# A fused attention and expert kernel: layer-norm statistics of x placed half a batch ahead, routing of a finished batch gathered in the first head group

## The reference, cut to what matters

```python
def _layernorm(x, axis=-1, eps=1e-05):
    m = jnp.mean(x, axis=axis, keepdims=True)
    v = jnp.var(x, axis=axis, keepdims=True)
    return (x - m) / jnp.sqrt(v + eps)
...
scores = jnp.einsum('bhqd,bhkd->bhqk', q, k) * scale
attn = jax.nn.softmax(scores, axis=-1)
out = jnp.einsum('bhqk,bhkd->bhqd', attn, v)
...
vals, idx = jax.lax.top_k(probs, K)
gates = mask / (jnp.sum(mask, axis=-1, keepdims=True) + EPS)
h = jax.nn.gelu(jnp.einsum('bsd,edh->besh', x, W1) + b1, approximate=False)
y = jnp.einsum('bse,besd->bsd', gates, jnp.einsum('besh,ehd->besd', h, W2) + b2)
...
x = x + xattn(_layernorm(x), ctx)
x = x + ffn(_layernorm(x))
```

## Time and profile before

| what | value |
|---|---|
| time, median of 3 runs | 816.91 us |
| lowest, highest | 812.75 us, 820.35 us |
| the profiled execution: its own time | 811.37 us |
| the profiled execution: its span | 809.6 us |
| PE busy | 751.9 us (93%) |
| DVE busy | 612.4 us (76%) |
| ACT busy | 455.7 us (56%) |
| POOL busy | 393.1 us (49%) |
| PE's mean granted clock | 0.966 |

### The profile page before, as it was taken

One profiled execution on the slowest core, in us unless ns is written; L12 is line 12 of the kernel. 1 busy time (PEld: TensorE's weight loads), 2 busy tenths in 40 slices (PEclk: granted clock), 3 DMA queues, 4 the chain that ended last, 5 costly groups with the idle time before them and its releaser, 6 DMA issues.

```text
span 809.6 us, 16188 instructions
## 1 busy us (share of the span) xinstructions
PE 751.9 (93%) x4634; PEld 449.7 (56%) x4634; DVE 612.4 (76%) x1123; ACT 455.7 (56%) x663; POOL 393.1 (49%) x354
## 2 busy tenths in 40 slices
PE   7689999999999999999999988759999989999995
PEld 3333434444444444444443433338999879998994
DVE  6586687788788788788788788536786887777674
ACT  1146766766766776776766756744345334444441
POOL 6406125628728728728725604243444455344444
PEclk9669999999999999999999999979999999999998
DMA  5765766757767767757757668874444555454441
GB/s 184 220 164 169 203 171 222 202 184 253 209 196 254 209 191 253 203 182 249 214 169 249 169 161 291 276 241 96 75 94 74 85 128 111 71 79 71 71 74 12
DMA packets 90667, 136.23 MB, mean 168 GB/s; under 512 B 15464, under 2 KB 49224, under 8 KB 90200
## 3 DMA queue, kind: packets, MB, share of 16 engines
q1 hardware_dynamic: 76456, 116.80, 48.0%
q0 software_dynamic: 13296, 17.09, 12.1%
q10 hardware_dynamic: 832, 1.31, 0.5%
HBM read 71.25 MB, written 64.04 MB: 167 GB/s over the span
## 4 chain that ended last, share of the span: by engine, by line
PE 66%; DMA 10%; DVE 10%; issue 5%; ACT 5%; POOL 2%; SPq 1%; POOLq 1%; DVEq 0%; ACTq 0%
PE ps_pv L1521 13%; PE ring L1508 9%; PE ring L1650 8%; PE ring L1668 8%; PE ring L1495 6%; DMA out<-y_sb,xs 6%; PE ps_x L1552 6%; DVE negm L1073 4%; PE ps_x L1570 4%; PE ps_x L1562 3%; ACT probs L1001 3%; PE ring L1659 2%; PE ps_x L1580 2%; PE ps_x L1539 1%; PE ps_pv L1641 1%
## 5 line engine op out<-in xcount | busy, mean ns | idle before, releaser
L1073 DVE TENSOR_REDUCE negm<-ring 128x2 f32<-128x1024 f32 x256 | 310.2, 1222 | 74.7 <-PE ring L1495 72.7
L1001 ACT ACTIVATE probs<-ring 128x1024 f32<-128x1024 f32 x256 | 260.4, 1023 | 91.1 <-PE ring L1508 90.1
L888 POOL DMA_INDIRECT out<-y_sb,xs x71 | 110.2, 1553 | 143.7 <-DMA out<-y_sb,xs 80.7
L1521 PE MATMUL ps_pv<-probs,v_aug 128*32 128x512 f32 x1024 | 139.0, 615 | 5.8 <-ACT probs L1001 5.8
L1508 PE MATMUL ring<-q_st,k_st 64*128 64x512 f32 x512 | 127.9, 499 | 7.0 <-DVE negm L1073 7.0
L1495 PE MATMUL ring<-k_st,q_st 64*128 64x512 f32 x512 | 110.5, 432 | 13.2 <-ACT probs L1001 4.9
L1508 PEld LDWEIGHTS ring<-q_st,k_st 64*128 64x128 f32 x512 | 48.5, 187 | 109.4 <-issue 76.9
L1035 ACT CAST xsT_hi<-ps_pv 128x256 fp32r<-128x256 f32 x71 | 26.4, 372 | 130.8 <-PE ps_pv L1641 130.8
L779 POOL DMA_INDIRECT xs_dram<-xg,rows x64 | 63.4, 991 | 52.7 <-DVEq L1241 32.1
L1668 PE MATMUL ring<-w_hi,hT_hi 128*128 x284 | 85.4, 301 | 0.1
L1668 PE MATMUL ring<-w_lo,hT_hi 128*128 x284 | 80.1, 282 | 0.0
(11 more groups left out here) (189 smaller groups left out, 1205.6 us busy)
## 6 DMA issues: line engine op xcount, KB each, us to landing
k_st<-k_dram SPq DMA_DIRECT2D x64, 192.0 KB
q_st<-q_dram SPq DMA_DIRECT2D x64, 192.0 KB
xs<-xs_dram SPq DMA_DIRECT2D x71, 132.5 KB, 2.4
k_dram<-qk_hi SPq DMA_DIRECT2D x32, 256.0 KB
q_dram<-qk_hi SPq DMA_DIRECT2D x32, 256.0 KB, 2.8
o_dram<-oT SPq DMA_DIRECT2D x32, 256.0 KB, 4.2
w_dram<-w_sb SPq DMA_DIRECT2D x12, 512.0 KB, 4.2
w_hi<-w_dram SPq DMA_DIRECT2D x11, 512.0 KB, 7.3
```

Source lines behind the costliest of these rows:

```text
L888: pool.indirect_dma_start(out=out, out_offset=bass.IndirectOffsetOnAxis(ap=xs[j % AHEAD][:, TOKEN:TOKEN + 1].bitcast(I32), axis=0), in_=y_ ...
L1001: nc.scalar.activation(probs[:, kt, 2 * jp:2 * jp + 2, :], ring[PLACE["ST", u, p] % RINGS][:], ACT.Exp).then_inc(exp_done, 1)
L1073: nc.vector.tensor_reduce(negm[:, v % 2, :, jp, kt], ring[PLACE["MX", v, p] % RINGS][:], AX.X, ALU.max, negate=True).then_inc(max_free, 1)
L1521: mm = nc.tensor.matmul(ps_pv[2 * DH * j:2 * DH * (j + 1), :], v_aug[:, kt, HPG * g + j, :], probs[:, kt, j, :], start=(kt == 0), stop=(kt ...
```

## The change

The statistics of batches 3 to 7 are computed by DVE one body earlier, in (2,6), (3,0) and (3,2) of the body three batches ahead instead of (0,3), (0,5) and (0,6) of the one two batches ahead; batch 2 stays in body 0. In bodies 2 to 6 the second choice goes from (0,4) to (0,3), the gates from (0,7) to (0,5), and PX (the matmuls and `route_rows`) from (1,2) to (0,6).

```diff
-LATE = {(1, 2): "PX"}
+LATE = {(0, 6): "PX"}
...
-LN = {(0, 3): "stats0", (0, 5): "stats1", (0, 6): "sums"}
+LN_FIRST = {(0, 3): "stats0", (0, 5): "stats1", (0, 6): "sums"}
+LN = {(2, 6): "stats0", (3, 0): "stats1", (3, 2): "sums"}
...
-ROUTE = {(0, 1): "softmax", (0, 2): "first", (0, 4): "second", (0, 7): "gates"}
+ROUTE = {(0, 1): "softmax", (0, 2): "first", (0, 3): "second", (0, 5): "gates"}
...
-                        if i + 2 < B and (g, p) in LN:
-                            ln(LN[g, p], i + 2)
+                        if i == 0 and (g, p) in LN_FIRST:
+                            ln(LN_FIRST[g, p], 2)
+                        if i + 3 < B and (g, p) in LN:
+                            ln(LN[g, p], i + 3)
```

## The result

The kernel after takes 825.88 us (median of 4 runs, 821.92 to 826.84) beside 815.91 for the kernel before on the same chip (4 runs, 812.75 to 820.35): ratio 1.0112, 95% interval 1.0075 to 1.0149. It is slower, by 10 us where 3 were forecast; the time lies within the range, near its upper end.

What follows compares the result with a forecast made beforehand. PE was taken to set the pace, DVE costing only where PE waits. Q1's wait +7.0, old waits -3.9 and statistics 0 gave +3.1 on the profiled execution, 820.0 us on the median; range 811.5 to 828.5.

Steps and rivals of the forecast that it cites:

- The wait at (1,5) goes: PE's one wait for a maximum in each of bodies 2 to 6, behind `route_rows`, disappears: 3.7 us won.
- Q1 waits for the bank, 1.4 us, for `gated` is held by `qk_lo`: At (0,7), Q1 waits for `row_of` to empty `ps_x`, DVE's gates meeting POOL's `qk_lo`: 1.4 us in each of five bodies.
- The power op may hold `xg` once more: POOL's power op, 1.04 us right behind `qk_lo`, holds `xg`: Q1's wait becomes 2.4 us in bodies 2 to 5.
- rival b: Longer wait at Q1 and PE's clock falling in it: 832.5 us, or 828.5 with the wait at 1.4; chance 0.17.
- The 3 us a body that the prediction left out of its sum: The skill's rule to the letter: xn's four parts hold `row_k` and `seen`, some 3 us more per body.
- PX at (0,6) with `route_rows` behind it is hidden: Before MT at (1,0), DVE's 3.2 us stays just hidden behind PE's some 3.6 us from Q1 on.
- `recT` stays covered: Reciprocal and SP's chain to `recT` move 1 us later, but DVE reaches `normalise` later still, so no cost.
- The statistics cost 0: At (2,6), (3,0), (3,2) the moved statistics fall in DVE's idle time: 0; without cover about 0.5 us a body.
- The sum of +3.1 us: Over five bodies: +7.0 for Q1's wait, -3.9 for old waits, statistics 0; profiled execution 811.37 to 814.5.
- second case of rival (b): Q1's wait stays 1.4 us but PE's clock falls after it: +11.6 us, 828.5.
- it decides from a wait of about 1.6 us: PE's clock falls after a wait at Q1 of about 1.6 us; full speed had been seen after 1.11.
- first case: Wait of 2.4 us at Q1 in bodies 2 to 5 with the clock falling in five bodies: +15.6 us, 832.5.

Runs made afterwards that it cites:

- second and third execution: Kernel after, unedited, run twice more beside the kernel before: 813.37 us, ratio 1.0070, and 814.43 us, ratio 1.0078.
- the statistics alone: Kernel before with only the statistics moved to (2,6), (3,0), (3,2), routing and PX left in place: 811.08 us, ratio 1.0031 to before.
- first execution of before: Kernel before, unedited, as first profiled: five stretches 305.3 us; median beside the first kernel after 815.91 us.
- stack loads later: Kernel after with SP's load_stack(i+1, 1) behind put_o, about 1 us later at (2,0): 816.94 us, ratio 1.0124 to before.
- routing alone: Kernel before with only second choice, gates and PX moved to (0,3), (0,5), (0,6), statistics left in place: 816.19 us, ratio 1.0100.

## Why the prediction was right or wrong

**The wait at (1,5) goes.** Right: 3.7 us in five bodies before, none after.

**Q1 waits for the bank, 1.4 us, for `gated` is held by `qk_lo`.** Right in place, cause and size: 1.38 to 1.44 us in all five bodies of all three executions, Q1 at 13.14 us after K0a in body 3 (242.54 - 229.40), where the prediction had 13.0 to 13.2 (242.97 to 243.14 less 229.97). The first comparison of the second choice was held too, 0.56 us for 0.19. Taking the ops out of `qk_lo`'s way removed the wait. In the second and third execution the stretches are 61.7 us, where the prediction had about 61.6 for bodies 2 to 6.

**The power op may hold `xg` once more (rival b, 2.4 us).** It did not: `xg`, started 0.12 us into it, took 0.19 us in bodies 2 to 5 of all three executions. For xn the prediction read too little out of its row. In body 4 of before `numT` took 0.69 us, but it had begun 0.08 us ahead of the fourth part of xn, and POOL was the one held, 1.70 us for 1.22; in body 3 it began 0.13 us behind the start of a part and took 0.96 (timelines of POOL and DVE):

```profile
247.29 1.22 POOL L802 TENSOR_SCALAR xn<-x_all,mv,rstd 128x256 f32<-128x256 f32 x1
247.42 0.96 DVE L1109 TENSOR_TENSOR numT<-numT,recT 128x512 f32<-128x512 f32 x1 [0.47 <-DMA recT<-r_dram]
...
308.88 1.70 POOL L802 TENSOR_SCALAR xn<-x_all,mv,rstd 128x256 f32<-128x256 f32 x1
```

`gated`, 0.22 us behind the first part, took 0.37 for 0.19. In all runs such a DVE op that began 0.1 to 0.4 us behind the start of a part was held to 0.4 us behind that start, and those that began later (`row_k` at 0.44 and 0.88, `numT` at 0.6 to 1.2) were not. So xn holds DVE for a third of its length, while the cast, `qk_lo`, `v_aug` and `w_lo` hold it to their end. The rule of the Trainium skill (SBUF — State Buffer, "Who interferes with whom") fits these four; against xn it has who blocks right and the length wrong, and the power op held nothing. The 3 us a body that the prediction left out of its sum did not come.

**PX at (0,6) with `route_rows` behind it is hidden.** Right: MT of (1,0) had no wait.

**`recT` stays covered.** Right, but just: with PX back at (1,2) it is 1.0 to 1.5 us late in bodies 2 to 5.

**The statistics cost 0.** In the three profiled executions of the kernel after this is what it was: `veps` at (3,2) took 0.40 us at most, and PE did not wait. But that was luck. The two `bn_stats` cost nothing, while `sums` ends with `veps`, which meets POOL's chain at (3,2): in body 2 of the second execution it came in the last `v_aug` and got through as `w_lo` began, 0.38 us; in the statistics alone it came one `v_aug` earlier and was held through `w_lo`, 3.36. I had bounded the cost by DVE's own work (1.8 us of it) and looked for meetings with POOL at the other end of the body only, though POOL's `v_aug` and `w_lo` stood in the same trace. Held for 2.8 to 3.5 us it costs PE 0.8 to 1.5 us, and more if the clock falls; it happened at this place in one or two bodies in each of four variants. Alone this part cost 0.3% (1.0000 to 1.0062).

**The sum of +3.1 us.** As a sum over the stretches it holds for the second execution of after: +3.4 against the first execution of before, +2.6 against the second (308.7 less 305.3 and 306.1). As a time it does not: the medians moved by 10.0 us on the first chip and 5.1 to 5.9 on the other occasions. In the first profile two terms are missing from it. The clock fell after waits of 1.4 us, which the prediction had as the second case of rival (b), with 11.6 us if in all five bodies; it was three of five, 5.0 us, and on other occasions none or one. That it decides from a wait of about 1.6 us did not hold: in the variants it fell after 1.06, 1.30, 1.33 and 1.43 us and did not after 1.24, 1.46 and twice 1.81. And ACT, DVE and POOL stood still together at (2,3), 5.0 us of PE's waits in bodies 2 to 6, which no case had. What makes either come in one execution and not in another of the same code stays open: shifting the scatters and the stack loads decided nothing, for the unedited kernel did not show the stand there either. The chance of 0.16 for a loss over 1% stood on rival (b), whose first case, a wait of 2.4 us, does not exist. That the first time, +10.0 us, lies within the range is partly luck: the range reached that far for the clock in all five bodies, and half of the way there was made by a stand that nothing had forecast.

**Not settled.** The 1.7 to 2.5 us between the medians and the stretches on the later occasions. A held `veps` or a fall of the clock in part of the executions would give that; a profile is of one execution each, and where the timed ones lost it is not seen. But each has its span and mean granted clock on record, and they point to the clock: (1 - clock) x span, an estimate of what the lower level took, is on average 26.8 and 26.7 us for the kernel after (8 and 7 executions, mean clock 0.967) and 24.4 for before beside it (21 and 20, 0.970), and the rest of the span differs by 2.8 and 3.9 us. So some 2.4 us of the difference goes with the clock (the scatter leaves about 1 us of doubt), and the rest is near what the stretches give.

## What to carry to other kernels

When a unit is moved to an earlier slot, list who uses its buffer next and what stands ahead of its reader on the reader's engine: here a wait of 0.4 to 1.2 us for a double buffer was traded for one of 1.4 for a single bank. Lay the moved ops, the tiny ones too, over the other engine's timeline as well: a DVE op of 0.17 us took 3.5 us behind POOL's chain, and moving it to where POOL is idle, with the gates ahead of `qk_lo`, turned +0.7% into -0.35%. That such an op met nothing in one execution does not say that it is safe: here tenths of a microsecond decided. Where the same code varies by more than the effect sought, profile it again before explaining a stall that one execution shows.

## What the runs showed of the hardware that was not expected

- A DVE TENSOR_SCALAR of 128x4 in SBUF stands behind several POOL ops in a row, not behind one: 3.12 us over the rest of `v_aug` and all of `w_lo`, to 343.97, where `w_lo` ends at 343.93 (stack loads later, body 4).
- A wait of PE of 1.4 us was followed by 3.4 us at the lower clock in 3 of 5, 0 of 5 and 1 of 5 bodies of three executions of one program. Each fall cost 1.6 to 1.7 us. The length of the wait alone does not decide: a fall followed one of 1.06 us (stack loads later) and none followed two of 1.81 (routing alone).
- A POOL TENSOR_SCALAR of 128x256 (xn, 1.22 us) holds a two-input DVE op only until 0.4 us behind its own start; when the DVE op began first, POOL's took up to 1.74 us.
- ACT, DVE and POOL stood together for 1 to 2.5 us at the same place, to a step, of five successive bodies in one execution, and in none of the other twelve.
